# A four-layer attention and expert kernel whose last stage is rebuilt as a pipeline of nine-slot periods

## Chip, cores and metric

One core of one Trainium2 chip runs the whole kernel. The metric is device time in microseconds (us). It is a single launch; all weights and constants come from HBM.

## What is computed

The reference is two transformer layers with post-norms on an input of 4 batches x 1024 positions x 128 features. The changed stage computes the second layer: attention over the four batch rows of one position (16 heads of 8, logits are negative squared distances), then a top-2-of-16 mixture of experts with a shared expert, each followed by a residual and a norm.

```python
x = _layernorm(x + _L0_attn_ref(...))      # 16 heads of 64, causal, alibi
x = _layernorm(x + _L0_ffn_ref(...))       # top-1 of 8 experts
x = _layernorm(x + _L1_attn_ref(...))      # the changed stage begins here
x = _layernorm(x + _L1_ffn_ref(...))
# _L1_attn_ref, per position and head, over the 4 batch rows s, t:
q = x @ w_q; logits = -(|q_t|^2 + |q_s|^2 - 2 q_t.q_s) / sqrt(8); a = softmax_s(logits)
out = (sum_s a[t, s] * (x_s A) v) @ out_w.T + out_b
# _L1_ffn_ref: sigmoid router, top 2 of 16, weights normalised, expert width 64
return x + shared(x) + sum(weight * expert(x))
```

## The kernel before

The kernel has four stages, one behind the other. Stages one to three (first attention, its output and norms, routing of the first experts and the net on gathered rows) are not touched and end near 1447 us. The last stage (from line 1436) is written out by hand for each engine; all engines run their own list in order and meet by semaphores.

A chunk is 128 positions of all four batches, so a 128x512 tile; there are TT = 8 chunks. For one chunk c the stage does this:

- arrival: VectorE adds the gathered expert output yin to X (L1691), takes the statistics of the norm (L144 to L152), GpSimd raises the variance to the power -1/2 (L167), VectorE applies mean and root (L157) into x2;
- attention: TensorE turns x2 (L1530), ScalarE copies it to SBUF as xts (L1617), TensorE projects queries and values into QV (L1539), ScalarE copies them to qv (L1623), VectorE takes the six pair differences (L1706), ScalarE squares (L1629), VectorE sums to distances (L1714), ScalarE takes Exp (L1634), VectorE copies the six weights to both halves of wf (L1719, L1720), sums and inverts them (L1723, L1726), and `weigh` (L1679, L1685) multiplies values by weights and reduces, once per batch row t; L1735 divides by the sums (o1n). TensorE turns the result and forms Y1 (L1546, L1551); VectorE adds the residual (L1746) and norms it (into xn, copied to X at L1752);
- router: TensorE turns xn (L1556) and forms the logits (L1562), ScalarE takes Exp (L1651), VectorE picks the first and second expert (`first_of`, L1106 to L1114) and forms three bf16 parts of the weights (L1785, L1788), TensorE turns them (L1568), ScalarE copies them to comb1 (L1656);
- net: nine steps j of 128 hidden units (two experts each). G and U (L1586, two matmul passes each) on TensorE, Silu on ScalarE (L1663), raw = sg * U on VectorE (L1794), M, which spreads the routing weights over the hidden units (L1594), hid = raw * M on VectorE (L1800), and down into Y (L1576) on TensorE;
- end: ScalarE copies Y to ys (L1669), TensorE turns it (L1604), VectorE adds twice X (L1806), statistics, GpSimd pow, apply into X, and SP stores the chunk (L1519).

`slots` gives the order. It walks c = 0 to 8 and, inside, q = 2 to 23; `after(c, q)` issues the attention and router of chunk c at fixed q, `second(c - 1, j)` issues net step j of the chunk before at the q of SECOND_AT, and `second_end(c - 1)` closes that chunk. So two chunks overlap. Shared buffers are the reason for most waits: the PSUM tensor W serves in turn as T, Y1, QV, R, C and T5, M is one bank, G, U, sg, raw and hid have two halves.

```python
SECOND_AT = (1, 4, 6, 8, 11, 13, 16, 19, 21)
...
    pe.wait_ge(hid5_ok, k)
nc.tensor.matmul(M[:], sel1[:, j, :], comb1[:, c % 2, :], start=True, stop=True).then_inc(m5, 1)
```

The wait quoted is the one between M of a step and hid of the step before, since M is a single bank.

Of the kernel before, what the change touches and what calls it, by code (L numbers as in the profile page):

```python
# [15 lines left out]
P = 128  # L16
# [82 lines left out]
def build(nc, a, out):  # L99
    ctx = ExitStack()  # L100
    with ctx:
# [24 lines left out]
        class Norm:  # L126


            def __init__(self, name, slots=1):
# [5 lines left out]
                self.vareps, self.rstd = sb(f"{name}_vareps", [P, slots, NB]), sb(f"{name}_rstd", [P, slots, NB])  # L135

# [16 lines left out]

            def vector_apply(self, dve, src, dst, n):
# [14 lines left out]
        norm = Norm("norm")  # L169
        norm1 = Norm("norm1")  # L170
# [1265 lines left out]
        with ExitStack() as sc:  # L1436
            def s4(name):
                return ctx.enter_context(nc.semaphore(name))

            n2, n3, n4 = (lambda c: TT // 2 + 2 * c), (lambda c: TT // 2 + 2 * c + 1), (lambda c: TT // 2 + c)  # L1440
# [6 lines left out]
            hid = sb("hid", [P, 2, CH], F32, sc)  # L1447
# [5 lines left out]
            wp = sb("wp", [P, NP, H1], F32, sc)  # L1453
# [4 lines left out]
            o1n = sb("o1n", [P, NB, D], F32, sc)  # L1458
# [41 lines left out]
            SECOND_AT = (1, 4, 6, 8, 11, 13, 16, 19, 21)  # L1500

            def slots(after, second, second_end):

                for c in range(TT + 1):
                    for q in range(2, 24):
                        if c < TT:
                            after(c, q)
                        if c and q in SECOND_AT[1:] + (2,):
                            second(c - 1, max(SECOND_AT.index(q) if q in SECOND_AT else 0, 0))
                    if c:  # L1510
                        second_end(c - 1)
# [11 lines left out]
            def _(pe):  # L1523
                def after(c, q):
                    if q == 5:
                        pe.wait_ge(norm.done, n2(c) + 1)
                        if c:
                            pe.wait_ge(c_ok, c)
# [383 lines left out]
```

## Time and profile before

| | us |
|---|---|
| median of 3 runs | 1947.53 (1941.84 to 1954.14) |
| profiled execution | 1947.45 |
| its span, first to last instruction | 1945.7 |
| TensorE matmul busy in the span | 1656.2 (85%) |
| VectorE / ScalarE / GpSimd busy | 1088.6 / 757.8 / 574.1 |
| mean granted TensorE clock | 0.899 of full |

The span is what the profiler saw between the first and the last instruction; the device time has 1.75 us around it. A busy time counts an engine's instructions, not its waits. The granted clock is 1.0 for 2.4 GHz and 0.5 for 1.2 GHz.

### The profile page before, as it was taken

What the parts mean: (1) busy time and instruction counts of PE and PEld (TensorE: products, weight loads), DVE (VectorE), ACT (ScalarE), POOL (GpSimd) and SP (SyncE); (2) the same over time, 40 slices, a digit from 0 to 9 for tenths busy, and PEclk for the clock granted to TensorE, in tenths of its full rate; (3) what the DMA queues carried; (4) which work ended last, traced back from release to release, by engine and by line L of the source; (5) the groups of instructions that cost most, each with busy time, mean ns of one, the idle gap of its engine ahead of it and who ended that gap; (6) DMA issues with size and microseconds to landing.
All of it is one profiled execution on the core that took longest, in us unless ns stands there. A gap on an engine that the chain in (4) does not pass through costs nothing. (4 is left out here: it accounts for less than half of the span.)

```text
span 1945.7 us, 28499 instructions
## 1 busy us (share of the span) xinstructions
PE 1656.2 (85%) x8973; PEld 777.5 (40%) x8974; DVE 1088.6 (56%) x2591; ACT 757.8 (39%) x1250; POOL 574.1 (30%) x557
## 2 busy tenths in 40 slices
PE   5899999999999999999999999647964677776777
PEld 2344444444444444443444444345642233232332
DVE  4454665565565555656556547562225766666674
ACT  2445445445444545445444453203422222232231
POOL 4244253253353353353452441160021001110000
PEclk8799999999999999999999999758976777887788
DMA  3602022022022022022021000131110000000000
GB/s 95 184 1 63 1 63 74 1 63 63 2 63 74 1 63 63 1 63 63 1 63 48 17 4 1 48 122 46 47 40 6 6 6 11 11 11 6 0 6 11
DMA packets 106705, 73.63 MB, mean 38 GB/s; under 512 B 5249, under 2 KB 100761, under 8 KB 106318
## 3 DMA queue, kind: packets, MB, share of 16 engines
q1 hardware_dynamic: 104526, 67.76, 11.4%
q0 software_dynamic: 2048, 4.20, 0.7%
q8 instruction: 73, 1.20, 0.3%
q14 instruction: 58, 0.48, 0.1%
HBM read 24.23 MB, written 47.71 MB: 37 GB/s over the span
## 5 line engine op out<-in xcount | busy, mean ns | idle before, releaser
L718 ACT ACTIVATE P<-S,keyb 128x386 f32<-128x386 f32 (+7 forms) x512 | 296.7, 630 | 387.9 <-PE S L514 387.8
L510 PE MATMUL S<-QT,KT 64*128 64x512 f32 (+5 forms) x1792 | 391.0, 492 | 9.5 <-DVE KT L856 7.3
L1036 POOL TENSOR_TENSOR rn<-nm,half 128x12 f32<-128x12 f32 x128 | 295.6, 2314 | 109.0 <-DVE nm L793 109.0
L1052 POOL TENSOR_SCALAR_AFFINE_SELECT P<-P 128x256 f32<-128x256 f32 (+1 forms) x256 | 156.5, 612 | 533.5 <-ACT P L718 533.4
L891 DVE TENSOR_TENSOR Psum<-Psum,P 128x1796 f32<-128x1796 f32 (+7 forms) x256 | 279.2, 1091 | 38.0 <-PE O L534 17.2
L534 PE MATMUL O<-P,V 128*64 128x512 f32 (+5 forms) x1536 | 255.5, 436 | 3.4 <-POOL P L1052 3.4
L510 PEld LDWEIGHTS S<-QT,KT 64*128 64x128 f32 (+1 forms) x1792 | 162.4, 183 | 202.2 <-issue 193.4
L167 POOL TENSOR_TENSOR norm_rstd<-norm_vareps,half 128x4 f32<-128x4 f32 x32 | 32.7, 1023 | 463.8 <-DVE norm_vareps L152 463.7
L405 PE MATMUL W<-xT,wts 128*128 128x512 f32 x256 | 147.1, 672 | 9.4 <-DVE QT L852 6.9
L514 PE MATMUL S<-GQ,GK 64*128 64x512 bf16 (+5 forms) x896 | 153.8, 310 | 0.0
L913 DVE TENSOR_TENSOR part<-W,rden 128x512 f32<-128x512 f32 x128 | 82.5, 686 | 92.6 <-PE W L582 92.6
L1576 PE MATMUL Y<-hid,dw 128*128 128x512 f32 x144 | 90.5, 714 | 41.5 <-DVE hid L1800 40.5
L534 PEld LDWEIGHTS O<-P,V 128*64 128x64 f32 (+1 forms) x1536 | 79.9, 135 | 110.9 <-issue 96.5
L718 ACT ACTIVATE Psum<-S,keyb 128x1024 f32<-128x1024 f32 x64 | 67.8, 1111 | 138.1 <-PE S L514 70.6
L1663 ACT ACTIVATE sg<-G 128x512 f32<-128x512 f32 (+1 forms) x72 | 42.8, 595 | 163.4 <-PE U L1586 163.3
L670 ACT COPY qkraw<-W 128x512 f32<-128x512 f32 x128 | 75.1, 587 | 64.5 <-PE W L405 64.5
L1586 PE MATMUL G<-XT,gw 128*128 128x512 f32 x144 | 94.1, 741 | 0.0
L800 DVE COPY V<-W 128x512 f32<-128x512 f32 x64 | 44.0, 687 | 84.8 <-PE W L433 84.8
L1794 DVE TENSOR_TENSOR raw<-sg,U 128x512 f32<-128x512 f32 (+1 forms) x72 | 49.0, 681 | 73.4 <-ACT sg L1663 73.4
L681 ACT ACTIVATE sq<-qkraw 128x512 f32<-128x512 f32 x128 | 80.6, 630 | 14.7 <-ACT qkraw L670 0.4
L1586 PE MATMUL U<-XT,uw 128*128 128x512 f32 x144 | 81.9, 652 | 0.0
L852 DVE SCALAR_TENSOR_TENSOR QT<-qkraw,scl,W 128x512 f32<-128x512 f32 x64 | 47.6, 743 | 60.6 <-PE W L468 60.2
(219 smaller groups left out, 2235.9 us busy)
## 6 DMA issues: line engine op xcount, KB each, us to landing
xg<-zero SPq DMA_DIRECT2D x16, 1216.0 KB, 6.9
yg<-zero SPq DMA_DIRECT2D x16, 1216.0 KB, 10.6
wts<-in_w_qkv SPq DMA_DIRECT2D x16, 384.0 KB, 3.8
gu<-in_gu SPq DMA_DIRECT2D x1, 2816.0 KB, 9.5
xb<-xg SPq DMA_DIRECT2D x40, 64.0 KB, 1.8
yg<-yb SPq DMA_DIRECT2D x40, 64.0 KB, 1.6
X<-in_x SPq DMA_DIRECT2D x4, 512.0 KB, 4.4
wo<-in_w_out SPq DMA_DIRECT2D x16, 128.0 KB, 2.3
```

Of the source, the lines that this page charges most:

```text
L405: nc.tensor.matmul(W[BANK[k]][:], wt[:, r, at:at + P], xT[:, n // NG % 2, NNULL + 512 * c:NNULL + 512 * c + 512], start=True, stop=True).t ...
L510: nc.tensor.matmul(S[hh][0:m, at + c:at + c + w], KT[d, r, p, jt * P:jt * P + m], QT[d, r, p, Q0[jt] + c:Q0[jt] + c + w], start=True, stop ...
L514: last = nc.tensor.matmul(S[hh][0:m, at + c:at + c + w], GK[d, jt * P:jt * P + m], GQ[d, r, p, Q0[jt] + c:Q0[jt] + c + w], start=False, st ...
L534: last = nc.tensor.matmul(O[hh * DH:(hh + 1) * DH, lo:hi], V[0:m, r, jt, (2 * p + hh) * DH:(2 * p + hh + 1) * DH], probs(p, jt)[0:m, hh, l ...
L681: nc.scalar.activation(sq[:, j, :], raw[:, c, j, :], ACT.Square).then_inc(sq_ok, 1)
L718: nc.scalar.activation(probs(p, jt)[0:m, hh, 0:n], S[hh][0:m, at:at + n], ACT.Exp, bias=keyb[0:m, r, (2 * p + hh) * NKT + jt:(2 * p + hh) ...
L891: nc.vector.tensor_tensor(x, x, probs(p, jt)[0:m, :, 0:NQ[jt]], ALU.add).then_inc(add_ok, 1)
L913: nc.vector.tensor_tensor(part[:, half_, hh], W[hh][:].rearrange("p (u d) -> p u d", u=4), rden[:, p, :, 2 * half_ + hh].unsqueeze(2).broa ...
L1036: nc.gpsimd.tensor_tensor(rn[:, c, u], nm[:, c, u], powers, ALU.pow).then_inc(rn_ok, 1)
L1052: nc.gpsimd.affine_select(own, own, [[0, 2], [1, w]], ALU.is_ge, 0.0, base=NNULL if jt == 0 else 0, channel_multiplier=-1).then_inc(cut, 1)
L1576: nc.tensor.matmul(Y[:], dw1[0:ROWS[j], j, :], hid[0:ROWS[j], (NJ1 * c + j) % 2, :], start=j == 0, stop=j == NJ1 - 1).then_inc(dn5, 1)
L1586: last = nc.tensor.matmul(o[k % 2][0:n, :], w[:, j * P:j * P + n], XT[:, c % 2, :], start=True, stop=True)
```

## The change

The last stage is put in another order and some of its work moves between engines. Period u now holds, in nine slots (one per net step), the attention of chunk u, the router of chunk u - 1, the net of chunk u - 2 and the last norm of chunk u - 3. Periods run from u = -1 to 10.

- Order: each engine has a function `slot(u, j)` in place of `after`, `second` and `second_end`; `down` runs two steps behind G and U (LAG = 2, it was one), also over the border of a chunk; hid has three buffers for it. G and U wait for raw of two steps before (prod_ok) instead of hid.
- Norms: GpSimd also multiplies the negated mean by the root (`pool_shift`), and ScalarE applies the norm as Identity with scale and bias from SBUF (`scalar_apply`), four activations of 128x128; VectorE negates the mean (`vector_shift`). The norm behind the attention writes X directly (no xn, no copy).
- Attention weights: ScalarE's Exp writes both halves of wf directly, six activations in place of one and twelve VectorE copies. VectorE divides the weights (wn, 128x256) rather than the result (128x512), and `weigh` runs twice over two batch rows each: one product of 1024 elements and two adds in place of two products and two strided reductions.
- Router: the logits are formed from XT, so the second copy of the turned rows (xts) goes. Its Exp stands directly behind the six of the attention on ScalarE.

The diff, cut to its core:

```diff
+            def pool_shift(self, pool, n):
+                pool.wait_ge(self.var, n + 1)
+                nc.gpsimd.tensor_tensor(self.rstd[:, 0], self.vareps[:, 0], half[:, 0, 0:NB], ALU.pow).then_inc(self.root, 1)
...
+                pool.wait_ge(self.neg, n - self.since + 1)
+                hold(pool)
+                nc.gpsimd.tensor_tensor(self.shift[:], self.minus[:], self.rstd[:, 0], ALU.mult).then_inc(self.moved, 1)
+            def scalar_apply(self, act, src, dst, n):
+                act.wait_ge(self.moved, n - self.since + 1)
+                for b in range(NB):
+                    last = nc.scalar.activation(dst[:, b, :], src[:, b, :], ACT.Identity, bias=self.shift[:, b:b + 1],
+                                                scale=self.rstd[:, 0, b:b + 1])
...
-            SECOND_AT = (1, 4, 6, 8, 11, 13, 16, 19, 21)
...
+            LAG = 2
+            def periods(slot):
+                for u in range(-1, TT + 3):
+                    for j in range(NJ1):
+                        slot(u, j)
...
+                def gate_up(c, j):
+                    wait_some(pe, prod_ok, k - 1)
...
+                def share(c, j):
+                    wait_some(pe, hid5_ok, k)
...
+                def slot(u, j):
+                    k = NJ1 * (u - 2) + j
+                    if live(u - 2):
+                        gate_up(u - 2, j)
+                    if j == 0:
+                        if live(u - 1):
+                            form(u - 1)
+                        if live(u - 2):
+                            combine(u - 2)
+                    elif live(u - 2):
+                        share(u - 2, j)
+                    if 0 <= k - LAG < KS:
+                        down(k - LAG)
+                    if j == 0 and live(u):
+                        rows_turned(u)
...
+                    if j == 1 and live(u):
+                        project(u)
+                    if j == 2 and live(u - 3):
+                        last_turned(u - 3)
...
+                def exponentials(c):
+                    act.wait_ge(dist_ok, c + 1)
...
+                        nc.scalar.activation(wf[:, t, t + 1:NB, :], w, ACT.Exp, scale=-(DH1 ** -0.5))
+                        last = nc.scalar.activation(wf[:, t + 1:NB, t, :], w, ACT.Exp, scale=-(DH1 ** -0.5))
...
+                    nc.vector.tensor_tensor(prod[:, :, 0:2], prod[:, :, 0:2], prod[:, :, 2:4], ALU.add).then_inc(half_ok, 1)
...
+                    nc.vector.tensor_tensor(o1[:, 2 * g:2 * g + 2], prod[:, :, 0], prod[:, :, 1], ALU.add).then_inc(o1_ok, 1)
...
+                    if j == 4 and live(u + 1):
+                        arrive(u + 1)
+                    if j == 6 and live(u):
+                        weigh(u, 1)
+                    if j == 8 and live(u - 1):
+                        weights(u - 1)
+                    if live(u - 2):
+                        gated(u - 2, j)
+                    if j == 0 and live(u - 1):
+                        joined(u - 1)
+                    if live(u - 2):
+                        shared(u - 2, j)
+                    if j == 2 and live(u - 3):
+                        ended(u - 3)
+                    if j == 4 and live(u - 1):
+                        logits(u - 1)
+                    if j == 5 and live(u):
+                        shares(u)
+                        weigh(u, 0)
```

Names of the changed kernel that the text uses: form is Y1, combine is C, share is M, gated is raw, shared is hid, joined is the residual and statistics behind the attention, ended the same for the last norm, arrive the sum and statistics of a new chunk.

VectorE, from the weights of the attention to the next net step, before (W3 and M3 are PSUM, sg is Silu's output):

```order
L1723 TENSOR_REDUCE den<-wf 128x64
L1726 RECIPROCAL den<-den 128x64
L1679 TENSOR_TENSOR prod<-qv,wf 128x512
L1685 TENSOR_REDUCE o1<-prod 128x128
L1679 TENSOR_TENSOR prod<-qv,wf 128x512
L1685 TENSOR_REDUCE o1<-prod 128x128
L1794 TENSOR_TENSOR raw<-sg,U30 128x512
L1800 TENSOR_TENSOR hid<-raw,M3 128x512
```

and the same place after:

```order
L1936 TENSOR_TENSOR hid<-raw,M3 128x512
L1846 TENSOR_REDUCE den<-wf 128x64
L1849 RECIPROCAL den<-den 128x64
L1851 TENSOR_TENSOR wn<-wf,den 128x256
L1860 TENSOR_TENSOR prod<-qv,wn 128x1024
L1865 TENSOR_TENSOR prod<-prod 128x2x256
L1868 TENSOR_TENSOR o1<-prod 128x256
L1860 TENSOR_TENSOR prod<-qv,wn 128x1024
L1865 TENSOR_TENSOR prod<-prod 128x2x256
L1868 TENSOR_TENSOR o1<-prod 128x256
L1927 TENSOR_TENSOR raw<-sg,U30 128x512
L1936 TENSOR_TENSOR hid<-raw,M3 128x512
```

Before, the four batch rows were weighed two and two with a net step between them; now both halves stand in one piece between hid of slot 5 and raw of slot 6.

ScalarE, around Exp, before:

```order
L1629 ACTIVATE sqd<-dif 128x768
L1663 ACTIVATE sg<-G31 128x512
L1634 ACT_TABLE_LOAD
L1634 ACTIVATE wp<-dist 128x96
L1663 ACT_TABLE_LOAD
L1663 ACTIVATE sg<-G30 128x512
```

and after, in slot 4 and at the head of slot 5:

```order
L174 ACTIVATE X<-xs,norm1_shift,norm1_rstd 128x128 x4
L1766 ACTIVATE sg<-G31 128x512
L1729 ACT_TABLE_LOAD
L1729 ACTIVATE wf<-dist 128x48
L1730 ACTIVATE wf<-dist 128x3x16
L1729 ACTIVATE wf<-dist 128x32
L1730 ACTIVATE wf<-dist 128x2x16
L1729 ACTIVATE wf<-dist 128x16
L1730 ACTIVATE wf<-dist 128x16
L1752 ACTIVATE sc1<-sc1 128x64
L1766 ACT_TABLE_LOAD
L1766 ACTIVATE sg<-G30 128x512
```

The two pairs of loads per chunk (the second stood around L1651) have become one pair, which also holds the router's Exp.

TensorE, from the last net step of a chunk into the next chunk, before:

```order
L1594 MATMUL M<-comb,sel 128x512
L1568 MATMUL W<-idb,w 51x128 x4
L1576 MATMUL Y<-hid,dw 128x512
L1604 MATMUL W<-idf,ys 128x128 x4
L1586 MATMUL G<-XT,gw 128x512
L1586 MATMUL U<-XT,uw 128x512
```

and after:

```order
L1638 MATMUL M<-comb,sel 128x512
L1646 MATMUL Y<-hid,dw 128x512
L1580 MATMUL W<-idf,o 128x128 x4
L1629 MATMUL G<-XT,gw 128x512
L1629 MATMUL U<-XT,uw 128x512
L1589 MATMUL W<-ow,ots 128x128 x4
L1618 MATMUL W<-idb,w 51x128 x4
L1646 MATMUL Y<-hid,dw 128x512
L1562 MATMUL W<-idf,x 128x128 x4
```

The turned routing weights (from w) are now behind G and U of their own chunk's first step, and the turn of ys has moved into the next period.

## Rows read from the trace of the kernel before

**Rows 1.** Stretches: us, busy (instructions) of PE, PEld, DVE, ACT, POOL; PEclk, DMA share, GB/s.

```profile
1447.70:1492.00 44.30, 11.13 (x37) 8.33 (x38) 24.35 (x82) 5.92 (x9) 8.72 (x9) 0.54 0.05 12
...
1609.40:1670.45 61.05, 45.27 (x108) 19.57 (x108) 38.57 (x114) 16.09 (x23) 6.92 (x7) 0.78 0.03 9
...
1906.20:1938.60 32.40, 30.52 (x67) 10.32 (x66) 15.43 (x32) 5.95 (x10) 1.01 (x1) 0.95 0.02 9
```

**Rows 2.** VectorE timeline: start, us, engine, line, operation, wait before it.

```profile
1447.67 0.69 DVE L1691 TENSOR_TENSOR X<-X,yin 128x512 f32<-128x512 f32 x1 [7.37 <-DMA yin<-yg,place]
...
1477.21 0.69 DVE L1746 TENSOR_TENSOR y<-W,y 128x512 f32<-128x512 f32 x1 [3.43 <-PE W L1551]
...
1491.76 0.69 DVE L1691 TENSOR_TENSOR X<-X,yin 128x512 f32<-128x512 f32 x1
...
1906.13 0.69 DVE L1806 SCALAR_TENSOR_TENSOR xs<-X,W 128x512 f32<-128x512 f32 x1 [4.51 <-PE W L1604]
```

**Rows 3.** TensorE timeline, down behind the sums of the attention.

```profile
1639.91 2.07 PE L1576 MATMUL Y<-hid,dw 128*128 128x512 f32 x2 [3.35 <-DVE hid L1800]
```

**Rows 4.** Short stretches around two waits of TensorE, columns as in rows 1.

```profile
1636.60:1639.80 3.20, 0.00 (x0) 0.00 (x0) 3.13 (x6) 0.60 (x1) 0.00 (x0) 0.99 0.00 0
1639.90:1649.60 9.70, 7.58 (x18) 4.14 (x19) 7.35 (x13) 0.59 (x1) 0.00 (x0) 0.50 0.00 0
1676.10:1678.60 2.50, 0.00 (x0) 0.01 (x1) 2.33 (x10) 0.60 (x1) 1.18 (x2) 1.00 0.17 63
```

**Rows 5.** TensorE timeline, the projection, and one net step with no other work.

```profile
1501.08 1.99 PE L1539 MATMUL W<-w1q,xts 128*128 128x256 f32 x8 [0.68 <-ACT xts L1617]
...
1919.64 1.13 PE L1586 MATMUL G<-XT,gw 128*128 128x512 f32 x2
...
1921.47 1.02 PE L1576 MATMUL Y<-hid,dw 128*128 128x512 f32 x2
...
1922.74 1.12 PE L1586 MATMUL G<-XT,gw 128*128 128x512 f32 x2
```

**Rows 6.** Groups of the last stage, VectorE: count, busy us, mean ns, idle before.

```profile
L1685 DVE TENSOR_REDUCE o<-prod 128x128 f32<-128x512 f32 x32 | 32.7, 1022 | 1.1
L1679 DVE TENSOR_TENSOR prod<-qv,wf 128x512 f32<-128x512 f32 x32 | 21.4, 669 | 0.0
...
L1706 DVE TENSOR_TENSOR dif<-qv 128x256 f32<-128x256 f32 x8 | 3.3, 418 | 0.0
```

**Rows 7.** VectorE timeline: router picks and weights (around one net step), then a norm.

```profile
1659.00 0.20 DVE L1761 TENSOR_SCALAR sc<-sc 128x64 f32<-128x64 f32 x1 [0.16 <-ACT sc L1651]
...
1665.74 0.20 DVE L1785 CAST w<-wt 128x68 bf16<-128x68 f32 x1
...
1674.88 0.69 DVE L1691 TENSOR_TENSOR X<-X,yin 128x512 f32<-128x512 f32 x1
...
1677.07 0.68 DVE L1794 TENSOR_TENSOR raw<-sg,U 128x512 f32<-128x512 f32 x1
```

**Rows 8.** ScalarE timeline around the load of the Exp table.

```profile
1630.75 0.58 ACT L1663 ACTIVATE sg<-G 128x512 f32<-128x512 f32 x1
1631.35 1.28 ACT L1634 ACT_TABLE_LOAD   x1
1632.65 0.28 ACT L1634 ACTIVATE wp<-dist 128x96 f32<-128x96 f32 x1
```

**Rows 9.** Groups of earlier stages, ScalarE, one operand from SBUF per partition each.

```profile
L718 ACT ACTIVATE P<-S,keyb 128x130 f32<-128x130 f32 x64 | 19.9, 361 | 13.3 <-PE S L514 13.3
...
L750 ACT ACTIVATE xnst<-S,gam 128x512 f32<-128x512 f32 x4 | 2.5, 692 | 0.0
```

**Rows 10.** Timeline of the end: the last sum, pow and apply of the norm.

```profile
1938.64 0.69 DVE L1806 SCALAR_TENSOR_TENSOR xs<-X,W 128x512 f32<-128x512 f32 x1 [2.55 <-PE W L1604]
...
1941.00 1.01 POOL L167 TENSOR_TENSOR norm_rstd<-norm_vareps,half 128x4 f32<-128x4 f32 x1 [31.50 <-DVE norm_vareps L152]
1942.04 1.12 DVE L157 TENSOR_SCALAR X<-xs,norm_mv,norm_rstd 128x128 f32<-128x128 f32 x4 [1.12 <-POOL norm_rstd L167]
```

More of the change, by code:

```diff
@@ L1498, in build, with live, wait_some @@
                 s4("x_ok5"), s4("m5"), s4("st_out"))
-            SECOND_AT = (1, 4, 6, 8, 11, 13, 16, 19, 21)
[L1502 to L1511, printed above, removed]
+            LAG = 2
+            KS = NJ1 * TT
+            def live(c):
+                return 0 <= c < TT
+            def periods(slot):
+                for u in range(-1, TT + 3):
+                    for j in range(NJ1):
+                        slot(u, j)
+            def wait_some(engine, signal, count):
+                if count > 0:
+                    engine.wait_ge(signal, count)
             block = sc.enter_context(nc.Block())
@@ L1572, in down, with rows_turned @@
-                def down(c, j):
-                    if j == 0 and c:
-                        pe.wait_ge(ys5_ok, c)
-                    pe.wait_ge(hid5_ok, NJ1 * c + j + 1)
-                    nc.tensor.matmul(Y[:], dw1[0:ROWS[j], j, :], hid[0:ROWS[j], (NJ1 * c + j) % 2, :], start=j == 0,
-                                     stop=j == NJ1 - 1).then_inc(dn5, 1)
-                def second(c, j):
+                def rows_turned(c):
+                    pe.wait_ge(norm.done, n2(c) + 1)
+                    wait_some(pe, c_ok, c - 1)
+                    wait_some(pe, ots_ok, c)
+                    for b in range(NB):
+                        last = nc.tensor.transpose(T[:, b, :], x2[:, b, :], idf[:])
+                    last.then_inc(x2_mm, 1)
@@ L1673, in _ @@
+                periods(slot)
             @block.vector
             def _(dve):
[L1675 to L1686 removed]
@@ L1815, in _ @@
                 dve.wait_ge(init, 2)
-                slots(after, second, second_end)
+                nc.vector.memset(wf[:], 1.0).then_inc(init, 1)
+                periods(slot)
             @block.gpsimd
@@ L1830, in _ @@
                 get_chunk(1)
-                for c in range(TT + 1):
-                    if c < TT:
-                        norm.pool(pool, n2(c))
-                        if c + 2 < TT:
-                            get_chunk(c + 2)
-                        norm.pool(pool, n3(c))
-                    if c:
-                        norm1.pool(pool, n4(c - 1))
+                periods(slot)
 def SHALF(jt):
```

530 lines of the change are left out of this document (285 added, 245 removed).

## Prediction

> **What bounds the kernel now.** I read the page first, for its engine totals and its 40 slices: TensorE is nearly full until slice 27, and the last ten slices, where the changed stage lies, have every engine partly idle and a granted clock that moves. So the next view is the stage by stretches [rows 1]. The first chunk alone takes 44.3 us and TensorE works 11 us of it. A full period (attention of one chunk, net of the chunk before) takes 61.05 us with TensorE busy 45.3 at a mean clock of 0.78, VectorE 38.6, ScalarE 16.1. The net alone takes 32.4 us with TensorE busy 30.5 at 0.95. No engine fills a full period: it is a chain that changes hands.
>
> The stage begins at 1447.7; the seven full periods run from 1491.8 to 1906.1, 59.2 us each [rows 2]. So stage = 44.1 + 7 x 59.2 + 32.5 (to the last xs at 1938.6) + 7.1 = 498.1 us, ending with the span at 1945.7.
>
> Where TensorE waits: down (Y) waited 3.35 us for VectorE's hid, behind the sums of the attention [rows 3]. The clock went with it: in the 3.2 us without matmuls it was still 0.99, in the next 9.7 us it was 0.50 (1.2 GHz), though TensorE was busy 7.6 of them; a wait of 2.5 us at 1676 left it at 1.00 (2.4 GHz) [rows 4]. The second such wait is on the two picks of the router. So a period pays for its waits, and again at half clock.
>
> With no wait, G, U, Y and M of one slot take 3.10 us at full clock, start to start [rows 5]: nine slots are 27.9 us. TensorE's whole work of a period is 45.3 x 0.78 = 35.3 us at full clock, so some 7 us are projections and transposes (the 8 projection matmuls took 1.99 [rows 5]). I take 35.0.
>
> **The change, part by part.** In a full period now: attention of chunk u, router of u-1, net of u-2, last norm of u-3, spread over nine slots. VectorE's own work first, from 38.6 us:
> - weigh: four products of 512 at 0.67 and four strided reductions at 1.02 go, and the final scaling of 512. With the gaps that is 4 x 1.65 + 0.7 = 7.3. In their place twice (product of 1024, add of 512, add of 256). From 0.67 at 512 and 0.42 at 256 [rows 6] an element costs 0.98 ns, so 1.17 + 0.67 + 0.42 + gaps = 2.4 each, 4.8, plus 0.42 for wn. Above, the product could be 2 x 0.67 (+0.2 each).
> - three norms are applied by ScalarE: 3 x 1.12 off VectorE [rows 10]; the copy of xn to X goes (0.4), the twelve copies into wf go (0 to 0.2 each, the small row of [rows 7]; 1.0 in all), three small negations come (0.2 at most, 0.1 behind others).
> Sum: 38.6 - 7.3 + 5.2 - 3.4 - 1.4 + 0.3 = 32.0 busy, 33.5 with the gaps between dependent instructions.
> - ScalarE: 12 activations of 128x128 with two pointer operands. One of 128x130 with one pointer is 0.36; a 128x512 with one is 0.69 against 0.58 without [rows 8, 9], so a second pointer adds 0.1: 0.46 each, four of them 1.7 (1.1 below, overlapped by 0.1 and with no second pointer; 2.8 above, at the 128x512 duration). It is idle 45 us of 61 now [rows 1], and each apply has two slots before its user. Six Exp of at most 0.28 replace one: about 1.0. Table loads fall from four to two per period, 1.28 each. So 16.1 + 5.1 + 0.7 - 2.6 - 0.6 (one xts copy) = 18.7 busy, under half of the period.
> - GpSimd: one more small multiply per norm, between nothing and the 1.01 of the pow [rows 10]; hidden, since norm2's user comes two slots (6 us) later. If that cover were gone it would put 1 us per period on the path.
> - SP and the gathers: the same transfers, issued a period earlier or later; the stores wait for ScalarE instead of VectorE. Nothing on the path but the last one.
>
> Now what ends last, walked through one period, t = 0 at the end of G,U of slot 0, full clock:
> TensorE has form, combine, down, rows turned, M (3.6), then slot 1 (3.1) and the projection (2.0), then G,U of slot 2 (1.8): t = 10.5. Silu 0.6: raw of slot 2 starts at 11.2. From here VectorE is the later one. raw+hid take 1.35, a norm's sum and statistics 2.2 [rows 7] and 0.1 for the negation: hid(2) 12.5, last norm 14.8, distances (768 elements, 0.95) 15.8, hid(3) 17.1, arrival of the next chunk 19.4, hid(4) 20.7, logits 21.0. Then a wait: the sigmoid's Exp 0.25, the load back to Silu 1.28, Silu 0.6 [rows 8], and two hand-offs: raw(5) at 23.2. hid(5) 24.6, shares 1.5 (three small instructions at 0.42 and gaps), both weighs 4.8, hid(6) at 32.3.
> TensorE meanwhile runs unbroken to G,U of slot 7: seven slots 21.7 + 6.5 of the other groups = 28.2. M(7) needs hid(6): it stands 4.1 us. In [rows 3, 4] the clock fell within a wait of 3.35 us and did not in one of 2.5, so I count on the fall. For the stretch at half clock behind it I take 4 us, a loss of 2.0: less than half of the 9.7 us of [rows 4], since in those TensorE was idle again for 2.1 us and here nothing stops it (nothing below; above the 9.7 us, a loss of 4.9). What is left of 35.0 is 6.8: 32.3 + 6.8 + 2.0 = 41.1. Some ten hand-offs between engines at 0.05 to 0.1 make 42.0. The picks and weights of slots 6 to 8 (6.9 us less one net pair of 1.35, 5.6 us [rows 7]) lie beside that low-clock stretch, so the router's wait goes; what is late next is weigh.
>
> The Trainium skill ("ScalarE: Activation LUTs", section "What ACT_TABLE_LOAD costs") has about 1380 ns of drain behind every 1283 ns load. The trace disagrees: the load began 0.02 us after the activation before it ended, and the Exp began 1.30 us after the load began [rows 8]. By the page two switches would put 2.8 us more before raw(5), 17 us over six periods, and the sum at 1842; by the row it is 1825.
>
> The stage's sum:
> - Fill: one attention, from arrival to y, takes 29.5 us [rows 2]. Two in sequence are 59, less the arrival, statistics and norm of the second (2.2 + 2 + 1.1), done beside the first: 53 until the first full period (44 below, one chunk as now; 59 above).
> - Six full periods (u = 2 to 7): 252.
> - u = 8, no attention: TensorE bound, 27.9 + 4.2 of the groups left = 32.5.
> - u = 9, net alone: 26.0 to the last G,U; Silu, raw, hid 2.0; down, copy, turn 2.4; sum and statistics 2.3; pow 1.05, multiply 0.5, apply 1.7; and 2.5 for the store as now [rows 10]: 38.5 (26.0 is eight slots and 1.3 of two small groups; copy 0.6 and turn 0.7 are as in the tail of the trace).
> Sum 376 against 498.1: 122 us less. The profiled execution took 1947.45 us (span 1945.7), at the median 1947.53 of the runs: 1947.4 - 122.4 = 1825.0 us.
>
> **Rivals.**
> A. The clock does not fall, because VectorE is quicker than walked and the stand short. For it: the stand of 2.5 us at 1676 left the clock alone [rows 4]. Against: 4.1 us is over the 3.35 in which it fell. Period 42 - 2.2 = 39.8, time 1812; without my hand-offs too, 1807.
> B. A second stand of some 3.3 us per period, at slots 2 to 4, where last norm, distances and arrival follow each other, or at raw(5) with the two table loads. Against: in the walk TensorE has work of its own in front of each of these. Price: 3.3 waited and half clock for 4 us on top, less what the first stand then loses: period 42 + 4 to 6, time 1855 (1849 to 1861).
> C. The load also waits for the activation before it to drain; by rows at most one 0.59 activation per switch, 1.2 per period: 1832. [...]
> D. Slower: the clock never comes back, because each period has one stand of 4 us and the work between the stands does not lift it. Then 35.0 is 70 us at half clock, period 70: 53 + 420 + 65 + 65 = 603, so 2050. It decides from a period of (498 - 124) / 6 = 62.4. Against: the clock rose again in each period of the trace, to a mean of 0.78, and to 0.95 with the net alone [rows 1].
> E. The four chunks bind each other (each engine runs its list in order, so one late wait holds all four) and the period stays at 61 [rows 1]: 6 x 61 = 366 in place of 252, 1939.
>
> **How the numbers follow.** Forecast 0.64, A 0.13, B 0.15, C 0.03, D 0.03, E 0.02. Predicted 1825. The range goes from A without hand-offs (1807, rounded to 1805) to B (1861, rounded to 1862). A measurement here tells about 1% from no change. Only E lies within that, and D above: faster 0.95, same 0.02, slower 0.03.
>
> **What would show it.** Right: xs to xs near 42 us in the middle periods; about 32 us VectorE and 19 us ScalarE busy in each; one TensorE wait per period, on hid behind weigh, 4 us, with the clock at 0.5 behind it; two table loads a period; net alone at 3.1 us a slot. The weigh products near 1.2 us. Wrong: M or G waiting in several slots, a mean clock under 0.8 in a period, an apply on ScalarE over 2 us that holds Silu, or a period over 48.

## The result, and the profile after

| us | before | after |
|---|---|---|
| median (lowest to highest) | 1948.07 (1941.84 to 1954.14) | 1815.55 (1815.06 to 1816.97) |
| profiled execution | 1947.45 | 1815.28 |
| its span | 1945.7 | 1813.4 |
| mean granted TensorE clock | 0.899 | 0.926 |

Both medians are of four runs, one more of the kernel before than the first table had. The ratio is 0.9329, with a 95% interval of 0.9298 to 0.936: 6.7% faster. The forecast was 1825.0 in a range of 1805 to 1862.

The stage is now measured from form to form (the Y1 matmuls, L1589), since one stands at the head of each period. It begins at 1448.00. The forms stand at 1500.44, 1538.81, 1579.84, 1620.84, 1661.81, 1702.78 and 1743.62; the last period, of the net alone, begins with combine at 1774.88, and the span ends at 1813.4. So the stage is 52.4 + 243.2 (six periods) + 31.3 + 38.5 = 365.4 us against the forecast 376, and 498.1 before.

Stretches of the changed kernel, with the columns of [rows 1]: the fill, a full period, three short stretches in it (the stand, in which TensorE waits, and what follows it), the period without an attention, and the rest.

```profile
1448.00:1499.50 51.50, 18.99 (x55) 13.41 (x56) 29.57 (x86) 16.05 (x40) 22.02 (x23) 0.53 0.08 21
...
1620.00:1661.00 41.00, 36.50 (x109) 15.79 (x108) 31.78 (x89) 17.97 (x38) 3.66 (x6) 0.92 0.02 7
1647.90:1652.50 4.60, 0.10 (x1) 0.00 (x1) 4.36 (x8) 0.60 (x1) 0.00 (x0) 0.86 0.00 0
1652.50:1657.00 4.50, 4.50 (x6) 1.31 (x7) 4.09 (x15) 0.00 (x0) 0.00 (x0) 0.50 0.00 0
1657.00:1660.00 3.00, 3.00 (x10) 0.91 (x9) 2.69 (x13) 0.59 (x1) 0.00 (x0) 0.83 0.00 0
1742.60:1774.00 31.40, 31.40 (x93) 12.93 (x92) 19.48 (x60) 12.91 (x24) 2.41 (x4) 1.00 0.02 9
1774.00:1813.40 39.40, 30.74 (x78) 10.98 (x76) 18.13 (x44) 10.18 (x20) 2.41 (x4) 0.93 0.04 14
```

Put the second row beside the full period of [rows 1], 61.05 us. TensorE's idle time fell from 15.8 to 4.5 us. What it lost to the clock fell from about 10 (45.3 busy at a mean of 0.78) to about 2.5 (36.50 busy, where a period at clock 1.00 has 34.05, in the third experiment below). So 11.3 of the 20 us are waits, and 7.5 to 9 are half clock: the work of the old period was 35.3 by the mean clock, but the matmuls are the same 108, and with 34.05 for them the old period lost 11.2 to the clock. VectorE fell from 38.6 to 31.8 busy, ScalarE rose from 16.1 to 18.0.

The 15.8 us before were four waits above all: 2.65, 3.35 and 1.44 us, for results of VectorE, and this one, the longest, for the routing weights.

```profile
1665.99 0.62 PE L1568 MATMUL W<-idb,w 128*51 128x128 bf16 x4 [4.81 <-DVE w L1785]
```

In the new period the weights of a chunk are ready when combine, at the head of the next period, wants them: its row at 1621.82 has no wait.

The one place in a full period where TensorE stands, from its timeline: M of slot 7, then the rest of the period to the next form.

```profile
1652.50 0.61 PE L1638 MATMUL M<-comb,sel 51*128 51x512 bf16 x1 [4.50 <-DVE hid L1936]
1653.04 2.07 PE L1646 MATMUL Y<-hid,dw 128*128 128x512 f32 x2
...
1658.38 0.39 PE L1638 MATMUL M<-comb,sel 51*128 51x512 bf16 x1
...
1661.81 1.05 PE L1589 MATMUL W<-ow,ots 128*128 128x128 f32 x8
```

Where [rows 3] had 3.35 us at down, M now waits 4.50, and the row names hid. The matmuls behind it show the half clock: Y takes 2.07 (as in [rows 3]) where it takes 1.12 at full clock, M 0.61 where it takes 0.39. The six full periods have this one wait each, 3.98 us in the first and 4.27 to 4.52 in the others. What VectorE did in the meantime:

```profile
1640.78 0.22 DVE L1884 TENSOR_TENSOR sc<-W,gb 128x64 f32<-128x64 f32 x1
1643.22 0.69 DVE L1927 TENSOR_TENSOR raw<-sg,U 128x512 f32<-128x512 f32 x1 [2.23 <-ACT sg L1766]
...
1644.55 0.57 DVE L1846 TENSOR_REDUCE den<-wf 128x64 f32<-128x256 f32 x1
...
1646.20 1.22 DVE L1860 TENSOR_TENSOR prod<-qv,wn 128x1024 f32<-128x1024 f32 x1
1647.46 0.69 DVE L1865 TENSOR_TENSOR prod<-prod 128x512 f32<-128x512 f32 x1
...
1648.72 1.22 DVE L1860 TENSOR_TENSOR prod<-qv,wn 128x1024 f32<-128x1024 f32 x1
...
1651.76 0.69 DVE L1936 TENSOR_TENSOR hid<-raw,M 128x512 f32<-128x512 f32 x1
```

raw of slot 5 waits 2.23 us for ScalarE. From there VectorE has no wait: hid, shares and both weighs stand before hid of slot 6, which ends at 1652.45, and M starts at 1652.50. One half of weigh is 2.5 us (0.67 + 1.02, twice, in [rows 6]: 3.4). ScalarE's side of that wait:

```profile
1636.63 1.65 ACT L174 ACTIVATE X<-xs,norm_shift,norm_rstd 128x128 f32<-128x128 f32 x4
1638.18 0.57 ACT L1766 ACTIVATE sg<-G 128x512 f32<-128x512 f32 x1
1638.78 1.28 ACT L1729 ACT_TABLE_LOAD   x1
1640.07 0.24 ACT L1729 ACTIVATE wf<-dist 128x48 f32<-128x48 f32 x1
...
1641.03 0.26 ACT L1752 ACTIVATE sc<-sc 128x64 f32<-128x64 f32 x1
1641.30 1.28 ACT L1766 ACT_TABLE_LOAD   x1
1642.59 0.60 ACT L1766 ACTIVATE sg<-G 128x512 f32<-128x512 f32 x1
```

The apply of a norm, four activations with two operands from SBUF, takes 1.65 us, and the six Exp 0.83 from the first start to the last end (1640.07 to 1640.90). This list has little room: the router's Exp at 1641.03 follows VectorE's logits, which end at 1641.00, and the six end only 0.13 us ahead of it. Both loads begin 0.01 to 0.03 us after the activation before them ended, and the next activation starts 1.29 after the load began, as in [rows 8]. The drain of about 1380 ns that the Trainium skill adds to a load ("ScalarE: Activation LUTs", section "What ACT_TABLE_LOAD costs") isn't in these rows either; its 1283 ns for the load itself is.

The end, beside [rows 10]:

```profile
1805.45 0.69 DVE L1945 SCALAR_TENSOR_TENSOR xs<-X,W 128x512 f32<-128x512 f32 x1 [2.60 <-PE W L1657]
...
1807.82 1.01 POOL L163 TENSOR_TENSOR norm_rstd<-norm_vareps,half 128x4 f32<-128x4 f32 x1 [20.39 <-DVE norm_vareps L154]
1809.03 0.20 POOL L168 TENSOR_TENSOR norm_shift<-norm_minus,norm_rstd 128x4 f32<-128x4 f32 x1 [0.20 <-POOL norm_rstd L163]
1809.26 1.65 ACT L174 ACTIVATE X<-xs,norm_shift,norm_rstd 128x128 f32<-128x128 f32 x4 [4.55 <-POOL norm_shift L168]
```

Here, and for the first chunk of the stage, nothing covers the new form of the norm. From the start of pow to the end of the apply it was 2.16 us before (1941.00 to 1943.16) and is 3.09 now (1807.82 to 1810.91), 0.9 us more.

### The profile page after: what moved, and what is told of

Its sections match the earlier page's. It is cut to its first block and busy times, and to the rows that moved or that the text cites. A ratio compares the mean times of both kernels' runs of the same rounds, so it can differ in the third digit from the quotient of the medians.

```text
span 1813.4 us, 28563 instructions
## 1 busy us (share of the span) xinstructions
PE 1602.4 (88%) x8973; PEld 756.6 (42%) x8974; DVE 1035.1 (57%) x2399; ACT 774.8 (43%) x1364; POOL 580.4 (32%) x581
## 5 line engine op out<-in xcount | busy, mean ns | idle before, releaser
L430 PE MATMUL W<-xT,wts 128*128 128x512 f32 x256 | 140.9, 644 | 9.8 <-DVE QT L877 7.2
L743 ACT ACTIVATE Psum<-S,keyb 128x1024 f32<-128x1024 f32 x64 | 67.8, 1110 | 137.2 <-PE S L539 69.8
L163 POOL TENSOR_TENSOR norm_rstd<-norm_vareps,half 128x4 f32<-128x4 f32 x24 | 24.9, 1037 | 289.3 <-DVE norm_vareps L154 289.3
L1646 PE MATMUL Y<-hid,dw 128*128 128x512 f32 x144 | 84.8, 673 | 0.0
L1629 PE MATMUL G<-XT,gw 128*128 128x512 f32 x144 | 81.9, 652 | 0.0
L1927 DVE TENSOR_TENSOR raw<-sg,U 128x512 f32<-128x512 f32 (+1 forms) x72 | 49.2, 683 | 54.4 <-ACT sg L1766 54.4
L539 PEld LDWEIGHTS S<-GQ,GK 64*128 64x128 bf16 (+1 forms) x896 | 55.0, 101 | 56.4 <-issue 41.3
## 6 DMA issues: line engine op xcount, KB each, us to landing
yg<-zero SPq DMA_DIRECT2D x16, 1216.0 KB, 10.6
```

The lines of the kernel that those rows point to most:

```text
L430: nc.tensor.matmul(W[BANK[k]][:], wt[:, r, at:at + P], xT[:, n // NG % 2, NNULL + 512 * c:NNULL + 512 * c + 512], start=True, stop=True).t ...
L539: last = nc.tensor.matmul(S[hh][0:m, at + c:at + c + w], GK[d, jt * P:jt * P + m], GQ[d, r, p, Q0[jt] + c:Q0[jt] + c + w], start=False, st ...
L743: nc.scalar.activation(probs(p, jt)[0:m, hh, 0:n], S[hh][0:m, at:at + n], ACT.Exp, bias=keyb[0:m, r, (2 * p + hh) * NKT + jt:(2 * p + hh) ...
L1629: last = nc.tensor.matmul(o[k % 2][0:n, :], w[:, j * P:j * P + n], XT[:, c % 2, :], start=True, stop=True)
L1646: nc.tensor.matmul(Y[:], dw1[0:ROWS[j], j, :], hid[0:ROWS[j], k % 3, :], start=j == 0, stop=j == NJ1 - 1).then_inc(dn5, 1)
```

## The experiments

The theory was that of the prediction: M of slot 7 stands for hid(6), which weigh delays, and the clock falls behind the stand. The rivals for each part stand in the expectations. The kernel before measured 1944.75 us beside the first four and 1944.9 beside the others.

The stages ahead are the same in all these kernels, yet in the profiled executions they don't end at the same time: the arrival of the first chunk, with which the changed stage begins, starts anywhere from 1441.98 to 1450.65 us. A difference of a few us between two medians can come from there. So the table has the stage itself beside each median, from that arrival to the end of the span, in the profiled execution: the fill up to the second form, the six full periods, and the rest.

| us | median | stage | fill | six periods | rest |
|---|---|---|---|---|---|
| changed kernel | 1815.55 | 365.4 | 52.4 | 243.2 | 69.8 |
| G and U of slot 7 twice | 1805.37 | 358.7 | 52.0 | 233.3 | 73.4 |
| second weigh moved | 1803.75 | 352.8 | 52.1 | 230.8 | 70.0 |
| VectorE's list spread | 1788.31 | 341.0 | 52.1 | 215.3 | 73.7 |
| old weigh | 1826.57 | 379.8 | 56.1 | 253.9 | 69.8 |
| spread, early arrival | 1788.26 | 340.5 | 50.1 | 215.1 | 75.3 |
| norms on VectorE | 1812.12 | 361.2 | 49.2 | 243.1 | 68.8 |
| order alone | 1835.06 | 387.2 | 54.8 | 263.4 | 69.1 |

The stage of the kernel before took 498.0 us by the same measure.

**The clock's part.** TensorE gets G and U of slot 7 twice, so that less of the stand is idle. Nothing else in the period changes.

```diff
-                    for w, o in ((gw1, G), (uw1, U)):
+                    for w, o in ((gw1, G), (uw1, U)) * (2 if j == 7 else 1):
```

> In the changed kernel TensorE issues G and U of slot 7 twice (same result, no new use). The stand before M of slot 7, 4.5 us, then holds 1.8 us of matmuls. Theory (the stand costs its own length and, through the granted clock, about 1.8 us more per period): the clock stays at 1.0, the period goes from 41.0 to 39.4, the time from 1815.5 to about 1806, although 1.8 us of TensorE work is added per net. Rival (only VectorE's list sets the period, the clock costs nothing): no change, 1815. Rival (TensorE's added work counts): 1826.

Measured: 1805.37 us, ratio 0.929 (0.9272 to 0.9308). With 1.7 us of matmuls more in each period (the stand went from 4.50 to 2.78) the six periods are 9.9 us shorter, and the stage 6.7, since the added matmuls also stand in the last two nets. The first two stretches lie 2 us behind M of slot 7 in two successive periods, the third is a whole period in which the clock stays up (columns as above); under them are those two Ms and the next one from TensorE's timeline, with the forms behind them.

```profile
1526.00:1528.00 2.00, 2.00 (x3) 0.48 (x3) 1.86 (x6) 0.00 (x0) 0.00 (x0) 0.50 0.00 0
...
1566.00:1568.00 2.00, 2.00 (x6) 0.57 (x5) 1.86 (x6) 0.59 (x1) 0.00 (x0) 1.00 0.01 4
...
1610.76:1649.15 38.39, 35.60 (x112) 16.03 (x111) 30.46 (x88) 17.94 (x38) 3.65 (x6) 1.00 0.02 7
```

```profile
1524.07 0.39 PE L1638 MATMUL M<-comb,sel 51*128 51x512 bf16 x1 [2.26 <-DVE hid L1936]
...
1532.39 1.05 PE L1589 MATMUL W<-ow,ots 128*128 128x128 f32 x8
...
1564.05 0.39 PE L1638 MATMUL M<-comb,sel 51*128 51x512 bf16 x1 [2.78 <-DVE hid L1936]
...
1570.78 1.05 PE L1589 MATMUL W<-ow,ots 128*128 128x128 f32 x8
...
1602.44 0.39 PE L1638 MATMUL M<-comb,sel 51*128 51x512 bf16 x1 [2.78 <-DVE hid L1936]
...
1610.76 1.05 PE L1589 MATMUL W<-ow,ots 128*128 128x128 f32 x8
```

The expectation had the clock at 1.0 in every period. It fell in three of the six, by turns, so periods alternate between 38.4 and 40.0 us. That the time came out as expected (1806) is partly luck: a fall costs more than the 1.8 us assumed, and only half of them went. At full clock M to form is 6.73 us (1564.05 to 1570.78), with a fall 8.32, and 9.31 in the changed kernel (1652.50 to 1661.81). So a fall costs 1.6 to 2.6 us, and it is the clock that this run gave back: the M itself came no earlier in its period (31.66 us after the form in both kernels).

**Where weigh stands.** The second half goes behind hid of slot 6 instead of ahead of its raw.

```diff
-                    if j == 6 and live(u):
-                        weigh(u, 1)
...
                     if live(u - 2):
                         shared(u - 2, j)
...
+                    if j == 6 and live(u):
+                        weigh(u, 1)
```

> Only the second weigh of a chunk moves, from before raw of slot 6 to behind hid of slot 6. Theory: the single stand of 4.5 us becomes two of about 2 and 2.7 us, neither with a fall of the clock; period 41.0 to 39.4, time about 1806. Rival (the sum of the waits counts and not where they stand, the clock falls all the same): 1815. If the second stand of 2.7 us brings the clock down: 1813 to 1817.

Measured: 1803.75 us, 0.9268 (0.9251 to 0.9285). The stand became two, at M of slot 7 and of slot 8; the rows are of two successive periods.

```profile
1644.07 0.39 PE L1638 MATMUL M<-comb,sel 51*128 51x512 bf16 x1 [1.98 <-DVE hid L1936]
1649.69 0.39 PE L1638 MATMUL M<-comb,sel 51*128 51x512 bf16 x1 [2.32 <-DVE hid L1936]
...
1683.97 0.39 PE L1638 MATMUL M<-comb,sel 51*128 51x512 bf16 x1 [2.00 <-DVE hid L1936]
1689.59 0.39 PE L1638 MATMUL M<-comb,sel 51*128 51x512 bf16 x1 [0.66 <-DVE hid L1936]
```

The position of weigh sets the stand, as the theory has it, but a move of one slot passes part of it on to the next M. The expected time (1806) came out, and the stage is 12.6 us shorter, but not because the clock stayed up: it fell in all six periods. In two it fell behind the second stand, and M of slot 8 to form took 5.12 us instead of 3.44. In the other four it fell behind the first, for instance here, behind a stand of 2.00 us that ended at 1567.67:

```profile
1567.70:1570.00 2.30, 2.30 (x4) 0.65 (x5) 2.23 (x4) 0.00 (x0) 0.00 (x0) 0.75 0.00 0
```

There the slow stretch only filled the wait in front of M of slot 8, 0.66 us instead of 2.32, and cost nothing: the two Ms are 5.62 us apart in both kinds of period.

**The rest of VectorE's list spread too.** Shares go ahead of raw(5), into the wait for ScalarE; each half of weigh stands behind a hid, and the picks move one slot down.

```diff
-                    if j == 6 and live(u):
-                        weigh(u, 1)
+                    if j == 5 and live(u):
+                        shares(u)
                     if j == 8 and live(u - 1):
+                        pick_other(u - 1)
                         weights(u - 1)
...
                     if j == 5 and live(u):
-                        shares(u)
                         weigh(u, 0)
-                    if j == 6 and live(u - 1):
-                        pick_one(u - 1)
+                    if j == 6 and live(u):
+                        weigh(u, 1)
                     if j == 7 and live(u - 1):
-                        pick_other(u - 1)
+                        pick_one(u - 1)
```

> VectorE's list is spread further: the sums and quotients of the weights go before raw of slot 5, into the 2.2 us that VectorE waits there for Silu; the first weigh stays behind hid of slot 5, the second goes behind hid of slot 6, the first pick behind hid of slot 7, the second pick into slot 8 before the weights. Theory (TensorE needs 35.0 us at full clock and VectorE 33.5): no stand over 1.5 us, clock 1.0, period about 38, time about 1797 to 1799. Rival (VectorE's waits only move to another slot): period over 39.5, time 1806 or more.

Measured: 1788.31 us (1787.13 to 1794.29), 0.9202 (0.9183 to 0.9221). The stage is 24.4 us shorter than in the changed kernel, where 17 to 19 were expected. A full period by its stretch, from form to form, and under it the waits of TensorE's matmuls in it from the timeline:

```profile
1565.80:1602.30 36.50, 34.05 (x108) 15.27 (x107) 31.57 (x90) 18.07 (x38) 7.56 (x10) 1.00 0.05 15
```

```profile
1568.06 0.41 PE L1618 MATMUL W<-idb,w 128*51 128x128 bf16 x4 [1.17 <-DVE w L1917]
1572.82 0.39 PE L1638 MATMUL M<-comb,sel 51*128 51x512 bf16 x1 [0.62 <-DVE hid L1936]
1595.25 0.39 PE L1638 MATMUL M<-comb,sel 51*128 51x512 bf16 x1 [0.32 <-DVE hid L1936]
1598.89 0.39 PE L1638 MATMUL M<-comb,sel 51*128 51x512 bf16 x1 [0.34 <-DVE hid L1936]
```

VectorE is as busy as before the edit (31.57 against 31.78), TensorE has the same matmuls, and yet the period is 36.5 instead of 41.0: one stand of 4.5 has become four of 2.45 in all, and the clock is 1.00 throughout. With it the other 2.5 us are gone. The six periods fell from 243.2 to 215.3 us (forms 1496.40 to 1711.65) and the fill stayed. The last 70 us grew by 3.9, nearly all of it in three waits that weren't there: 1.17 and 1.46 for the weights at the heads of the next two periods, and 1.06 at an M.

**The new weigh, taken back.** In the changed kernel the four products and four strided reductions return.

```diff
-                    nc.vector.tensor_tensor(prod[:, :, 0:2], prod[:, :, 0:2], prod[:, :, 2:4], ALU.add).then_inc(half_ok, 1)
...
+                    for t in (2 * g, 2 * g + 1):
...
+                            ALU.mult).then_inc(pr_ok, 1)
+                        dve.wait_ge(pr_ok, n + 1)
+                        nc.vector.tensor_reduce(o1[:, t, :], prod[:, t % 2].rearrange("p s n -> p n s"), AX.X,
+                                                ALU.add).then_inc(o1_ok, 1)
```

> One part undone: weigh is again four products of 512 and four strided reductions per chunk, in the new order, with the same two places. VectorE works 1.7 us more in the stretch that sets the end. Theory: the stand grows from 4.5 to 6.2 us, the period from 41.0 to 42.7, twice as much in the fill of two attentions: 1815.5 + 6 x 1.7 + 3.4 = 1829. Rival (the slots hide it): 1815 to 1818.

Measured: 1826.57 us, 0.9387 (0.9371 to 0.9403), 11 us more by the medians and 14.4 by the stage (10.7 in the six periods, 3.7 in the fill), where the theory had 13.6. The wait at M of slot 7 is that of the changed kernel with 1.8 us more:

```profile
1617.91 0.61 PE L1638 MATMUL M<-comb,sel 51*128 51x512 bf16 x1 [6.29 <-DVE hid L1936]
```

Two reductions of 1.02 in each half against two adds, 0.69 and 0.42, make (2 x 1.69 - 2.33) x 2 = 2.1 us of VectorE; 1.8 of it arrived at the stand.

**The arrival two slots earlier.** On top of the spread order, the arrival of the next chunk moves from slot 4 to slot 2, where VectorE waited 2.4 us for qv; GpSimd's step of it moves along.

```diff
+                    if j == 2 and live(u + 1):
+                        arrive(u + 1)
...
-                    if j == 4 and live(u + 1):
-                        arrive(u + 1)
```

> On top of the spread list: the arrival of the next chunk (sum and statistics, 2.2 us of VectorE) goes from slot 4 to slot 2, into the 2.4 us that VectorE waits for the projected queries before it takes the differences; GpSimd's list follows. Theory: VectorE's list was the bound (33.5 us and 3.2 us of waits in a period of 36.5); now TensorE is, with 34.05 us at full clock: period 34.3 to 34.8, time 1788 - 6 x 2 = 1776. Rival (the waits of VectorE are filled but move elsewhere, as the copy of the queries comes from TensorE in its own time): period 36 or more, time 1785 or more.

Measured: 1788.26 us, 0.9199 (0.9179 to 0.9219), the same as without the move; the expected 1776 was wrong, and the rival holds. VectorE did lose the wait, and got another one two net steps later:

```profile
1615.39 0.69 DVE L1927 TENSOR_TENSOR raw<-sg,U 128x512 f32<-128x512 f32 x1 [0.20 <-ACT sg L1766]
...
1622.74 0.69 DVE L1927 TENSOR_TENSOR raw<-sg,U 128x512 f32<-128x512 f32 x1 [1.51 <-ACT sg L1766]
...
1626.93 0.69 DVE L1927 TENSOR_TENSOR raw<-sg,U 128x512 f32<-128x512 f32 x1 [0.43 <-ACT sg L1766]
...
1641.09 0.20 DVE L1917 CAST w<-wt 128x68 bf16<-128x68 f32 x1
```

Of the expected order in time, raw(2) did not come earlier: it starts 12.5 us after the form (1602.86 to 1615.39), as ScalarE copies qv only when TensorE has projected. Then raw(4) waits 1.51 for a silu that stands behind the apply of the last norm on ScalarE. From raw(5) to the last part of the weights VectorE has no wait, 14.4 us, and combine waits for just that part (1.17 us again). By these rows the spread order is bound by a ring: combine and its successors on TensorE, projection, the copy of qv, VectorE's slots 2 to 8, combine. No run shortened a link of it, so that is read and not shown. Here, work moved from one of VectorE's places to another gave nothing.

**The norms back on VectorE.** The three applies return from ScalarE; the rest of the change stays.

```diff
-                def rows_normed(c):
-
-                    wait_some(act, yb_pre, c)
-                    wait_some(act, x2_mm, c)
-                    norm.scalar_apply(act, X[:, c], x2, n2(c))
...
+                        norm2.vector_apply(dve, y2, X[:, u - 1], u - 1)
...
-                        norm2.pool_shift(pool, u - 1)
+                        norm2.pool(pool, u - 1)
```

> One part of the change undone in the new order: VectorE applies the three norms (mean and root in one instruction), GpSimd's multiply and ScalarE's twelve activations go. Theory (VectorE's time counts only from raw of slot 2 to hid of slot 6, where the last norm's apply stands): 1.05 us per period, 6 x 1.05, with about nothing from the other two, less 1 us in the fill: 1820 to 1823. Rival (VectorE's whole list counts): 6 x 3.3, 1835. Rival (ScalarE's applies were in the way): under 1812.

Measured: 1812.12 us, 0.932 (0.93 to 0.9341), against 0.9329 of the changed kernel: no loss, where 5 to 8 us were expected. The six periods are as long as before the edit (243.1 against 243.2). One step of the expectation held: hid(6) came later, M(7) starts 32.54 us after the form (1620.44 to 1652.98) instead of 31.66, at a stand of 4.65.

```profile
1652.98 0.61 PE L1638 MATMUL M<-comb,sel 51*128 51x512 bf16 x1 [4.65 <-DVE hid L1922]
...
1661.66 1.05 PE L1589 MATMUL W<-ow,ots 128*128 128x128 f32 x8
...
1694.22 0.39 PE L1638 MATMUL M<-comb,sel 51*128 51x512 bf16 x1 [4.65 <-DVE hid L1922]
...
1702.54 1.05 PE L1589 MATMUL W<-ow,ots 128*128 128x128 f32 x8
```

What cancelled it was the clock: M to form is 8.68 and 8.32 here against 9.31, and 8.32 in four of the six periods. In the second pair M itself still ran at full clock (0.39), in the changed kernel it was at half (0.61). Why the full clock came back or left at another point isn't settled by this run. The stage as a whole is 4.2 us shorter than the changed kernel's: 0.9 ahead of the first form, where an apply has no cover, and 1.0 behind the last one; the 2.3 between the first two forms are mostly a projection at full clock (1.99 us instead of 3.78), which may be chance. So in the order as it stands ScalarE's applies are worth nothing in a full period and cost about 2 us at the ends. What they would be worth in the spread order, where the clock doesn't fall, was not tried.

**Order and operations apart.** First the new order with the old operations: norms on VectorE, the old weigh, one Exp and twelve copies. (The division stays on the weights, the logits from XT, and the copy into X doesn't return.)

```diff
-                        nc.scalar.activation(wf[:, t, t + 1:NB, :], w, ACT.Exp, scale=-(DH1 ** -0.5))
...
+                    nc.scalar.activation(wp[:], dist[:], ACT.Exp, scale=-(DH1 ** -0.5)).then_inc(wp_ok, 1)
...
+                    for k, (t, s) in enumerate(PAIRS):
+                        nc.vector.tensor_copy(wf[:, t, s, :], wp[:, k, :])
+                        last = nc.vector.tensor_copy(wf[:, s, t, :], wp[:, k, :])
```

> The order alone: the new order with the operations of before in the attention and the norms (norms applied by VectorE, weigh of four products and four strided reductions, one Exp and twelve copies on VectorE; only the quotients stay on the weights). In the stretch from raw of slot 2 to hid of slot 6 that is 1.05 + 1.7 + 1.0 us more. Theory: period 44.8, time 1815.5 + 6 x 3.8 + 5 = 1843; so of the 132 us the order gives about 104 and the operations 28. Rival (the operations made the order possible): period over 50, time over 1875.

Measured: 1835.06 us, 0.9441 (0.9421 to 0.9461). Period and stand:

```profile
1623.40:1667.80 44.40, 36.30 (x108) 15.77 (x108) 37.64 (x113) 13.14 (x20) 3.05 (x3) 0.88 0.02 6
```

```profile
1623.32 0.61 PE L1639 MATMUL M<-comb,sel 51*128 51x512 bf16 x1 [7.55 <-DVE hid L1923]
```

VectorE is busy 37.64 us of the period, nearly the 38.6 of [rows 1], yet the period is 44.4 and not 61.05. The stand grew from 4.50 to 7.55. So the order brought some 110 of the 129 to 133 us, and all new operations together 20 on top (110.8 and 21.8 by the stage). What belongs to which part of the order (the router a period behind, down two steps behind, the waits of G and U on raw) was not taken apart.

Then the reverse, the new weigh alone in the kernel before. It divides the weights, multiplies 1024 elements at once and adds; the order stays.

```diff
-                    nc.vector.tensor_reduce(o1[:, t, :], prod[:, t % 2].rearrange("p s n -> p n s"), AX.X,
-                                            ALU.add).then_inc(o1_ok, 1)
...
+                    nc.vector.tensor_tensor(prod[:, :, 0:2], prod[:, :, 0:2], prod[:, :, 2:4], ALU.add).then_inc(half_ok, 1)
```

> The operations alone, as far as weigh goes: the kernel before with the new weigh (quotients on the weights, one product of 1024 and two adds for two batch rows). VectorE works 1.9 us less per chunk, 0.4 of it in front of the hid for which down stands 3.35 us. Theory: 8 x 1.9 = 15 us less than the kernel before if the clock falls as it did (1930); each period in which the stand of 3.0 us no longer brings the clock down gives 4 us more, at most 30 in all (1900). Rival (the old order hides it): within 5 us of before.

Measured: 1935.87 us (1922.26 to 1941.0 in ten runs), 0.994 (0.9914 to 0.9966), 9 us less (6.7 by the stage in the profiled execution). A chunk has 4 x 1.69 + 0.7 = 7.5 us of VectorE removed and 2 x 2.33 + 0.42 = 5.1 added, 19 us in eight chunks; about half came through, less than the 15 us that the expectation had even without a gain in clock. The wait of down for hid went from 3.35 to 3.00 us in each of the seven periods, and in the profiled execution, one of the slower ones at 1940.81, the clock fell behind it every time (0.50 to 0.62 in the 4 us behind). The runs of this kernel spread over 1%, so the share is rough.

## Why the prediction was right, step by step

- **The mechanism** is the one walked through, and the runs bear it out: one stand per period, at M of slot 7, for hid(6) behind weigh, the clock at 0.5 behind it. The rows show 4.50 us for the 4.1 predicted. Moving weigh (second and third run) moved and dissolved the stand; more weigh (fourth) lengthened it by 1.8 of the 2.1 us that VectorE got.
- **The walk's times**, from the form: raw(2) at 10.6 (11.2 predicted), raw(5) at 22.4 (23.2), M(7) at 31.66 (32.3). The walk was 0.6 to 0.8 late everywhere before any allowance, and 0.6 of that is in its first piece: form to G of slot 1 took 3.13 us (3.6), the projection 1.83 (2.0). From raw(2) to M(7) it is 21.1 in both. The period is 41.0 or 40.8 where 42.0 stood. So the 0.9 us per period added for hand-offs weren't there; this is the term that was mis-sized. Without it the walk has 41.1, which is as near as that by some luck: M(7) 0.6 early and 0.5 more behind it cancel.
- **The clock loss** was set at 2.0 us and is 2.6 by M to form (9.31 - 6.73). So 6.8 + 2.0 was predicted behind M(7), and 6.73 + 2.58 is there. TensorE's work was taken as 35.0 and is 34.05; the 1.0 us too much lay ahead of M(7) (27.2 us where 28.2 stood). It didn't lengthen the period, because VectorE sets M(7), but it made the stand 4.1 where it is 4.5.
- **The costs of parts**: product of 1024 elements 1.22 (1.17), its two adds 0.69 and 0.42 (0.67 and 0.42); ScalarE's apply 1.65 (1.7); six Exp 0.83 (1.0); VectorE 31.8 busy (32.0); ScalarE 18.0 (18.7). GpSimd's multiply, which nothing before showed, takes 0.20 where 0.5 was taken within 0 to 1.01. Applies and multiply lay beside other work but at the head of the fill and in the tail. ScalarE's applies take 0.48 us each (0.46 in the sum) and overlap by 0.09. The Trainium skill ("ScalarE: Activation LUTs", section "What ACT_TABLE_LOAD costs") prices such an activation at 186 ns + 0.833 ns per element + 93 ns per operand from SBUF, with an overlap of 93; an estimate by that page is 479 ns each and 1.64 us for four, and the trace agrees.
- **The sum**: fill 52.4 (53), six periods 243.2 (252), u = 8 31.3 (32.5), the rest 38.5 (38.5). Of the 10.6 us that the stage is below its forecast, 8.8 are the six periods: about 1 us in each, as above, and 2.6 more in the first (38.4), which was counted as full though it has no last norm yet. Its M of slot 7 starts 30.05 us after the form instead of 31.66, and M to form is 8.32 instead of 9.31. So it lacks 1.6 us of the work ahead of the stand and lost 1.0 less to the clock. Three slips in the adding are small: the fill adds up to 53.7 and was entered as 53, u = 8 to 32.1 and was entered as 32.5, and the terms are 122.1 us less, not 122.4.
- **Why so much faster than 61 us** was right in direction and is now measured: the pipeline takes waits off TensorE first (15.8 to 4.5 us), and the half clock goes with them (10 or 11 to 2.5). The prediction named the wait for the router's picks second and without a size; it was the longest of the period (4.81), and with the order it is gone. Order without the new operations gives 110 us.
- **The rivals.** A (clock stays) holds for none of the six periods: M to form is 8.3 to 9.4 in all, never 6.73. With a price of 2.0 to 2.2 us it was near: the fall costs 1.6 to 2.6. B (a second stand) isn't there: where last norm, distances and arrival follow each other in slots 2 to 4, no M waits. C: the load doesn't wait for the activation before it to drain (0.01 to 0.03 us); two loads per period are in the 2.23 us that VectorE waits, as the walk had them. D: the clock came back in each period; in the one shown it was 0.50 from M at 1652.50 to 1657.00, and M of slot 8, 5.9 us behind that of slot 7, ran at full clock again (0.39). E is refuted by the period itself.

## What to carry to other kernels

When a list in fixed order feeds the tensor engine, ask where in the period the feeding engine's longest unbroken piece stands: between a period of 41.0 and one of 36.5 us its busy time didn't change, only the places of the pieces did. One stand is paid twice, as idle time and as half clock behind it. Here four short ones, 1.17 us at most, left the clock alone, while stands of 1.75 to 2.8 did so only at times. A fall costs nothing where its slow stretch ends in a wait that would have been there anyway. A walk made of start-to-start rows already holds the hand-offs (21.1 us from raw(2) to M(7), walked and measured), and the first and last periods are counted by what they lack.

## What was not expected of the hardware

- The length of a stand alone does not tell whether the clock falls. In one kernel (first run) it fell after a stand of 2.26 us, stayed at 1.00 after one of 2.78 (1564.05) and fell again after the next of 2.78 (1602.44), with the same matmuls around the last two. In the second run it stayed at 1.00 after 1.98 us (1644.07), fell after another of 1.98 and after one of 1.75, and was 0.73 in the 2.3 us after the one of 2.32. What a fall costs also varies between periods of one kernel: M to form takes 8.6 to 9.7 us in the fourth run, at the same wait of 6.29.
- A stand of 4.65 us could leave the next matmul at full clock (0.39 us for M, at 1694.22 of the sixth run) and drop the clock only behind it: M to form is then 8.32, as in the changed kernel's first period, where M also took 0.39, behind a stand of 3.98. With M at half clock it is 9.3 in the changed kernel, but 8.7 in the sixth run at 1652.98, so which matmul is the first at half clock isn't all of it. The difference of up to 1 us per period was worth as much as the norms' work on VectorE.
